# Turning one batch's normalised rows and folding the bias vectors in another way, in a gated attention kernel with experts

## What is computed

```python
qkv = jnp.einsum('bsh,oh->bso', hidden_states, w_qkv) + b_qkv
scores = jnp.einsum('bqh,bkh->bqk', q, k) / scaling
out = jnp.einsum('bsh,oh->bso', context, w_out) + b_out
...
logits = jnp.einsum('bsd,de->bse', x, router_w) + router_b
topk_vals, topk_idx = jax.lax.top_k(logits, TOP_K)
expert_out = jax.nn.silu(h)
out = jnp.einsum('bsd,df->bsf', combined, proj_w) + proj_b
return norm_w * (y / rms)
...
x = x + s * g
```

## Time and profile before

| | us |
|---|---|
| time, median of 3 runs | 485.66 (485.57 to 486.53) |
| the profiled execution's own time | 484.21 |
| its span, first to last instruction | 482.5 |
| TensorE busy in the span | 474.7 |
| VectorE, ScalarE, GpSimd busy | 315.7, 214.0, 217.6 |

### The profile page before, as it was taken

The page is one execution under the profiler, slowest core; times in us unless marked ns, Lnnn a source line. Parts: engine busy times, 40 slices in busy tenths (PEclk is TensorE's granted clock), DMA queues, the critical chain, the costliest instruction groups (busy, mean ns, idle before and its releaser), DMA issues.

```text
span 482.5 us, 7168 instructions
## 1 busy us (share of the span) xinstructions
PE 474.7 (98%) x2168; PEld 391.9 (81%) x2169; DVE 315.7 (65%) x471; ACT 214.0 (44%) x310; POOL 217.6 (45%) x318
## 2 busy tenths in 40 slices
PE   9999999999999999999999999999999999999995
PEld 7878777888888888888888888888888888888884
DVE  4965352776734446898888889753588665857653
ACT  3673563143230264644644444333655452554540
POOL 5685010007887859500400000664478873476234
PEclk9999999999999999999999999999999999999998
DMA  8956999956979599978789666996555874455412
GB/s 312 353 210 253 382 348 410 357 186 235 324 243 334 186 320 308 285 212 259 230 269 263 201 191 176 338 315 246 151 176 174 239 198 151 123 190 172 149 46 86
DMA packets 78192, 115.79 MB, mean 240 GB/s; under 512 B 6657, under 2 KB 36369, under 8 KB 78161
## 3 DMA queue, kind: packets, MB, share of 16 engines
q1 hardware_dynamic: 65072, 79.72, 52.5%
q0 software_dynamic: 6896, 23.36, 13.9%
q10 hardware_dynamic: 6192, 12.32, 7.3%
HBM read 66.09 MB, written 49.28 MB: 239 GB/s over the span
## 4 chain that ended last, share of the span: by engine, by line
PE 97%; DVE 1%; issue 1%; ACT 0%; DVEq 0%
PE ab L1662 22%; PE ab L1664 22%; PE ab L1663 22%; PE sc L1662 8%; PE sc L1664 7%; PE sc L1663 7%; PE tp L1668 2%; PE tp L1704 1%; PE tp L1763 1%; PE sc L1733 1%; PE sc L1774 1%; PE sc L1736 1%; PE ab L1686 0%; PE ab L1688 0%; DVE xt_l L1229 0%
## 5 line engine op out<-in xcount | busy, mean ns | idle before, releaser
L822 POOL DMA_INDIRECT y<-y_scratch,pos x32 | 33.3, 1042 | 77.7 <-DMA y_scratch<-yt_so 63.3
L1664 PE MATMUL ab<-W,st_l 128*128 x156 | 60.7, 389 | 0.0
L1663 PE MATMUL ab<-W,st_h 128*128 x156 | 60.7, 389 | 0.0
L1662 PE MATMUL ab<-W,st_h 128*128 x156 | 60.7, 389 | 0.0
L805 POOL DMA_INDIRECT rows_scratch<-xb,pos x32 | 31.2, 975 | 51.2 <-DVEq L1343 43.0
L1662 PE MATMUL sc<-xt_h,t_h 128*128 128x512 f32 x128 | 50.1, 391 | 0.0
L1664 PE MATMUL sc<-xt_h,t_l 128*128 128x512 f32 x128 | 49.9, 390 | 0.0
L1663 PE MATMUL sc<-xt_l,t_h 128*128 128x512 f32 x128 | 49.8, 389 | 0.0
L1081 ACT CAST st_h<-tp 128x512 fp32r<-128x512 f32 x39 | 22.9, 587 | 43.3 <-PE ab L1664 41.2
L1423 DVE TENSOR_REDUCE small<-sc 128x1 f32<-128x1024 f32 x16 | 19.5, 1221 | 24.7 <-PE sc L1664 24.4
L1664 PEld LDWEIGHTS ab<-W,st_l 128*128 128x128 f32 x156 | 29.3, 188 | 6.1
(11 more groups left out here) (286 smaller groups left out, 1227.4 us busy)
## 6 DMA issues: line engine op xcount, KB each, us to landing
rows_scratch<-xn ACTq DMA_DIRECT2D x3, 3328.0 KB, 20.1
xb<-in_expert_w POOLq DMA_DIRECT2D x6, 1024.0 KB, 10.1
xn<-rows_scratch SPq DMA_DIRECT2D x48, 128.0 KB, 3.1
xg<-rows_scratch SPq DMA_DIRECT2D x44, 128.0 KB, 3.1
y_scratch<-yt_own SPq DMA_DIRECT2D x20, 256.0 KB, 3.1
y_scratch<-yt_so SPq DMA_DIRECT2D x19, 256.0 KB, 3.1
p_scratch<-prob SPq DMA_DIRECT2D x9, 512.0 KB, 2.8
rows_scratch<-xs SPq DMA_DIRECT2D x16, 256.0 KB, 6.7
```

The lines of the kernel that those rows point to most:

```text
L822: pool.indirect_dma_start(y[:, q, :], None, y_d, bass.IndirectOffsetOnAxis(pos[:, GB * s + p:GB * s + p + 1], 0))\
L1662: nc.tensor.matmul(dst, lh, rh, start=start, stop=False)
L1663: nc.tensor.matmul(dst, lh, rl, start=False, stop=False)
L1664: return nc.tensor.matmul(dst, ll, rh, start=False, stop=stop)
```

## The change

Batch 1's rows are normalised in place (xb1), stay there for the scatter, and are stored to HBM as before. They aren't turned by TensorE: spread_pair, new on SP, waits for the stores of a pair and loads it back in four quarters, and turn_spread, new on VectorE, transposes blocks of 32 by 32 into tp. The scatter takes batch 1 first; eight loads to sent_rows are gone. The high and low halves of batch 1's last four tiles go to the room of the split key weights (turned_rows), so ScalarE waits with them until the folds are done. Two of the three clearing transfers are issued by SP behind spread_pair instead of by ScalarE. The expert weights' first loads wait for the last turn instead of the last normalised row, as they write the same buffer.

The bias vectors are made in another way: weigh_rows on VectorE adds up the rows of the query (key) weights, each chunk times its number of the other bias; GpSimd splits the sum in halves; sum_rows on TensorE multiplies a square of ones with both halves, so that every partition holds the whole vector; and pick on VectorE takes from it, with the identity, the number of each partition. The statistics of batch 1 are one turn earlier. The router's products of batch 0 now come ahead of those of batch 1.

```diff
...
+        def turned_rows(g):
+            w = slice(g % QB * P, (g % QB + 1) * P)
+            if g < GB:
+                return xt_h[:, :, g * P:(g + 1) * P], xt_l[:, :, g * P:(g + 1) * P]
+            if g < GB + QB:
+                return bt_h[:, :, w], bt_l[:, :, w]
+            return wk_h[:, :, w], wk_l[:, :, w]
...
-                sp.dma_start(rows_g[home(g)], xs[:, g % 4, :]).then_inc(xn_st[g % 4], 16)
+                sp.dma_start(rows_g[home(g)], xs[:, g % 4, :] if g < GB else xb1[:, g - GB, :])\
+                    .then_inc(xn_st[g % 4], 16)
+            def spread_pair(n):
+                g = GB + 2 * n
+                for k in (g, g + 1):
+                    sp.wait_ge(xn_st[k % 4], 16 * (k // 4 + 1))
+                for a in range(4):
+                    sp.dma_start(xb[32 * a:32 * (a + 1), 2 * n:2 * n + 2, :].rearrange("p t (r f) -> p (t r) f", r=4),
+                                 rows_q[home(g):home(g) + 2, a, :, :, :].rearrange("t s r f -> s (t r) f"))\
+                        .then_inc(x_in[n], 16)
             load_half(0)
-            for g in range(G):
+            for g in range(GB):
                 if g == 4:
                     load_half(1)
                 store_row(g)
+            for g in range(GB, GB + 4):
+                store_row(g)
+            for n in range(KC):
+                spread_pair(n)
+                if n < 2:
+                    store_row(GB + 4 + 2 * n)
+                    store_row(GB + 5 + 2 * n)
+            for n in (1, 2):
+                clear_slots(sp, n)
...
             def load_to_send(g):
-                if g >= GB:
-                    sp.wait_ge(sent[g % GB], 32)
-                sp.dma_start(sent_rows[:, g % GB, :], rows_g[home(g)]).then_inc(send_in[g % GB], 16)
+                sp.wait_ge(sent[g], 32)
+                sp.dma_start(sent_rows[:, g, :], rows_g[home(g)]).then_inc(send_in[g], 16)
...
+            link(pool.tensor_copy(ones_r[:, :], ones[:, :]))
+            for m in range(2):
+                pool.wait_ge(weighed, m + 1)
+                link(pool.tensor_copy(sums[m][:, 0, :], raw[m][:, 0, :]))
+                pool.tensor_tensor(sums[m][:, 1, :], raw[m][:, 0, :], sums[m][:, 0, :], ALU.subtract).then_inc(qk_split, 1)
+            pool.wait_ge(t_done, G)
...
-            for g in range(G):
-                pool.wait_ge(send_in[g % GB], 16 * (g // GB + 1))
+            for n in range(G):
+                g = (n + GB) % G
+                if n >= GB:
+                    pool.wait_ge(send_in[g], 16)
...
-                nc.scalar.activation(xs[:, g % 4, :], xbs[g // GB][:, g % GB, :], ACT.Identity, bias=shift[:, g:g + 1],
+                whole = xbs[g // GB][:, g % GB, :]
+                nc.scalar.activation(xs[:, g % 4, :] if g < GB else whole, whole, ACT.Identity, bias=shift[:, g:g + 1],
...
+                if g >= GB + QB:
+                    act.wait_ge(fold, 2 * KC)
+                high = turned_rows(g)[0]
...
             act.wait_ge(ln_done, 3)
-            for g in range(GB, GB + 4):
+            for g in range(GB, GB + 6):
                 normalise(g)
             fold_high(KC)
-            act.wait_ge(vecs, 2)
-            nc.scalar.copy(bias_rows, ab[0:2, :, :].rearrange("p a n -> p (a n)")).then_inc(rows_out, 1)
+            normalise(GB + 6)
+            act.wait_ge(qk_split, 6)
             hi(GB)
+            normalise(GB + 7)
             hi(GB + 1)
             fold_high(KC + 1)
-            normalise(GB + 4)
-            normalise(GB + 5)
             hi(GB + 2)
             hi(GB + 3)
             fold_high(KC + 2)
-            normalise(GB + 6)
-            normalise(GB + 7)
             fold_high(KC + 3)
-            act.wait_ge(rt_done, 1)
...
+            def weigh_rows(m):
+                other = bcols[:, 1 - m, :]
+                dve.wait_ge(qk_split, 4)
+                total = raw[m][:, 0, :]
+                link(vec.tensor_scalar(total, total, other[:, 0:1], None, ALU.mult))
+                for c in range(1, KC - 1):
+                    link(vec.scalar_tensor_tensor(total, raw[m][:, c, :], other[:, c:c + 1], total, ALU.mult, ALU.add))
+                vec.scalar_tensor_tensor(total, raw[m][:, KC - 1, :], other[:, KC - 1:KC], total, ALU.mult, ALU.add)\
+                    .then_inc(weighed, 1)
...
+            def turn_spread(g):
+                k = g - GB
+                dve.wait_ge(x_in[k // 2], 64 + 16 * (2 if k < 4 else 1))
+                dve.wait_ge(lo_done, g - 1)
+                vec.transpose(tp[:, g % 2, :, :].rearrange("p c (r s) -> p c r s", r=4),
+                              xb[:, k, :].rearrange("p (r q c) -> p c r q", r=4, c=KC)).then_inc(t_done, 1)
...
+            def pick(m, out):
+                each = picked[m].rearrange("p (c q) -> p c q", c=KC)
+                link(vec.tensor_tensor(each, ab[:, m, :].rearrange("p (q c) -> p c q", c=KC),
+                                       ident[:, :].unsqueeze(1).to_broadcast([P, KC, P]), ALU.mult))
+                return vec.tensor_reduce(out, each, AX.X, ALU.add)
...
+            def fold_query_bias():
                 dve.wait_ge(const, 6)
-                dve.wait_ge(vecs, 3)
-                two = lambda m: ab[:, 0, 2 * KC * m:2 * KC * (m + 1)].rearrange("p (c a) -> p c a", a=2)
-                vec.tensor_reduce(tb[:, :], two(0), AX.X, ALU.add).then_inc(pre_done, 1)
-                link(vec.tensor_reduce(rw[:, :, E], two(1), AX.X, ALU.add))
-                vec.tensor_reduce(rb_bc[:, E:E + 1], ab[:, 0, 4 * KC:5 * KC], AX.X, ALU.add).then_inc(pre_done, 1)
+                dve.wait_ge(vecs, 2)
+                link(vec.tensor_reduce(rb_bc[:, E:E + 1], ab[:, 1, 0:KC], AX.X, ALU.add))
+                pick(0, rw[:, :, E]).then_inc(pre_done, 1)
+                dve.wait_ge(pre_done, 2)
                 link(vec.tensor_copy(rw_hl[:, :, 0, :], rw[:, :, :]))
                 vec.tensor_tensor(rw_hl[:, :, 1, :], rw[:, :, :], rw_hl[:, :, 0, :], ALU.subtract).then_inc(pre_done, 1)
+            def fold_key_bias():
+                dve.wait_ge(vecs, 3)
+                pick(1, tb[:, :]).then_inc(pre_done, 1)
                 dve.wait_ge(pre_done, 4)
...
-                if 2 <= t < 6:
-                    n = t - 2
+                if 1 <= t < 5:
+                    n = t - 1
...
+            weigh_rows(0)
+            weigh_rows(1)
+            turn_spread(GB)
+            turn_spread(GB + 1)
             fold_low(KC)
             lo(GB)
+            turn_spread(GB + 2)
             lo(GB + 1)
+            turn_spread(GB + 3)
+            fold_query_bias()
             fold_low(KC + 1)
-            fold_biases()
             lo(GB + 2)
+            turn_spread(GB + 4)
             lo(GB + 3)
+            turn_spread(GB + 5)
             fold_low(KC + 2)
+            fold_key_bias()
             fold_low(KC + 3)
-            for g in range(GB + QB, G):
-                lo(g)
+            lo(GB + 4)
+            turn_spread(GB + 6)
+            lo(GB + 5)
+            turn_spread(GB + 7)
+            lo(GB + 6)
+            lo(GB + 7)
...
-            def bias_products():
-                for m, (high, low) in enumerate(((wk_h, wk_l), (wq_h, wq_l))):
-                    nc.tensor.matmul(ab[0:2, m, :], bc_hl[:, m, 0, :], high[:, 0, :], start=True, stop=False)
-                    for c in range(KC):
-                        nc.tensor.matmul(ab[0:1, m, :], bc_hl[:, m, c, 0:1], low[:, c, :], start=False, stop=False)
-                    for c in range(1, KC):
-                        last = nc.tensor.matmul(ab[0:2, m, :], bc_hl[:, m, c, :], high[:, c, :],
-                                                start=False, stop=(c == KC - 1))
-                last.then_inc(vecs, 1)
-            def turn_biases():
-                pe.wait_ge(rows_out, 1)
-                for n in range(2 * KC):
-                    nc.tensor.transpose(ab[:, 0, 2 * n:2 * n + 2], 
-                                        every_fourth(bias_rows[:, n // KC * D:(n // KC + 1) * D], n % KC), ident[0:2, 0:2])
-                nc.tensor.matmul(ab[:, 0, 4 * KC:5 * KC], ones[:, :], prod, start=True, stop=True).then_inc(vecs, 1)
...
+            def sum_rows(m):
+                pe.wait_ge(qk_split, 5 + m)
+                if m == 0:
+                    pe.wait_ge(ab_read, 2 + GB)
+                    nc.tensor.matmul(ab[:, 1, 0:KC], ones[:, :], prod, start=True, stop=True)
+                else:
+                    pe.wait_ge(pre_done, 2)
+                nc.tensor.matmul(ab[:, m, :], ones_r[:, :], sums[m][:, 0, :], start=True, stop=False)
+                nc.tensor.matmul(ab[:, m, :], ones_r[:, :], sums[m][:, 1, :], start=False, stop=True).then_inc(vecs, 1)
...
             pe.wait_ge(qk_split, 4)
             pe.wait_ge(pre_done, 1)
             fold_keys(FOLDS[0])
-            pe.wait_ge(ab_read, 2 + GB)
-            bias_products()
-            turn(GB)
-            turn(GB + 1)
             fold_keys(FOLDS[1])
-            turn_biases()
-            turn(GB + 2)
```

(17 more changed lines are left out.)

64 lines of the change are left out of this document (31 added, 33 removed).

## The result

| | kernel before | changed kernel |
|---|---|---|
| median (lowest to highest), us | 485.62 (485.23 to 486.53) | 490.12 (489.43 to 490.44) |
| ratio, 95% interval | | 1.0081 (1.0065 to 1.0097) |
| profiled execution, its span, granted clock | 484.21, 482.5, 0.997 | 489.43, 487.7, 0.989 |

The changed kernel is slower by 4.5 us by the medians and by 3.9 us by the ratio; the forecast was 3.8 us slower, 489.5. The spans of the two profiled executions differ by 5.2, and all of that is made in one stretch. The first fold starts at 45.99 (45.97 before); the scores start at 91.36 instead of 86.16; the attention's first product comes 22.4 us behind the scores in both kernels.

A forecast was written before the change was run, and what follows sets the result against it. TensorE's instruction row was taken as the bound: 8.0 us less work against 10.7 of waiting gave +2.65, the clock's fall added 1.1, so +3.8 on 485.66, 489.5 us; range 485.0 to 493.0.

The forecast's parts named there:

- 8.0 saved, 10.7 of waiting: TensorE before the scores: 8.0 us net less work against 10.7 us of new waits, scores 2.65 us later.
- The half of the turns: TensorE's four pairs of row-tile turns before the scores, about 1.05 us a pair, 4.2 us of work removed.
- the half of the bias vectors: TensorE's bias products (3.69 us) and bias-row turns with ones product (1.3) go; new products cost 1.2.
- T: Time the first pair of batch 1's rows is back from HBM: 56.7, bounds 54.8 and 61.6.
- The weighted sums: VectorE's two row sums from 47.5, 3.0 us each, done at 50.5 and 53.5; TensorE waits 0.8.
- The pick: VectorE's first bias pick, queued behind transposes, ends 8.4 us after T; TensorE idles 9.1 us until 65.1.
- The clock: Granted clock halves in TensorE's long wait; slow products behind it cost 2.0 us, adding 1.1 net.
- The wait of 0.9 for the third fold's low half: TensorE, second half of the logits: waits 0.9 us for VectorE, which has 6.1 us queued against TensorE's 5.2.
- The backlog of transfers: Rival: queued transfers delay the first probabilities' store and load at the attention, 1 to 3 us more, 491.5; 9 in 100.
- the end moves by what the scores move by: Sign in the profile after: the span's end shifts by the same amount as the start of the scores.
- The hidden round trip: Rival: weighted sums hide the trip, transposes start at 53.5, Q 3.2 us sooner, time 485.3; 14 in 100.
- The steady clock: Rival: the clock holds through TensorE's idle time, all else as forecast, 488.3; 15 in 100.

The follow-up runs named there:

- e5: Changed kernel's trip of batch 1's rows through HBM alone, bias vectors made as in the kernel before: 489.91 us, ratio 1.0077 to the kernel before.
- e8: e7 with VectorE's key pick behind the last fold's low half and TensorE's wait for it moved to the attention's key products: 481.69 us, ratio 0.9917.
- e9: Changed kernel without the 16 loads in quarters, transposes reading the buffer as it stands (results wrong): 485.15 us, ratio 0.9986 to the kernel before.
- e3: Changed kernel with 36 unused products in TensorE's long wait to hold the clock up: 491.27 us, ratio 1.0114 to the kernel before.
- e6: e3 with the 2 MB store of folded key weights issued behind the fourth probabilities' load: 488.48 us, ratio 1.005 to the kernel before.
- e7: e4 with sums in VectorE's pauses, statistics earlier, clears moved, folds, turns and picks reordered, key weights' store late: 484.29 us, ratio 0.996.
- e10: Changed kernel with both halves reordered: picks and low halves ahead of transposes, TensorE's batch 1 work last, late key weights' store: 482.5 us, ratio 0.9923.
- e1: Changed kernel with the first bias pick moved directly behind the weighted sums, ahead of the block transposes: 489.76 us, ratio 1.0085 to the kernel before.
- e12: e11 with its second clear cut from 13 tiles to 7, the rest on SyncE behind the loads in quarters: 479.39 us, ratio 0.9876.
- e11: e10 with the first tile's maximum ahead of routing, choices counted later, second clear issued from ScalarE in turn 5: 483.33 us, ratio 0.9945.
- e4: Kernel before with the bias half alone, batch 1 still turned by TensorE, clears where they were: 484.15 us, ratio 0.9966.
- e2: Changed kernel with the first clearing transfer also issued behind the loads in quarters: 497.7 us, ratio 1.0227 to the kernel before.

## Why the prediction was right, and where not

The mechanism was right: the work that leaves TensorE is outweighed by one long wait for a pick that stands behind the round trip. That the time came out so close is in part luck, as the next paragraphs show: most sizes missed to the same side, the trace moved by 5.2 us where 3.8 were forecast, and the medians moved by less than the traces.

**The balance.** "8.0 saved, 10.7 of waiting" was the argument. Measured: 10.5 of waiting (1.06 and 9.44; forecast 0.8, 9.1, 0.9) and 2.2 for the clock. The stretch of 45.4 less 10.5 and 2.2 is 32.7, so the work is 7.5 less than in the 40.2 before, not 8.0. Forecast: -8.0 + 10.7 + 1.1 = +3.8, where the 1.1 are a clock's price of 2.0 less 0.9 of waiting under it; in the trace: -7.5 + 10.5 + 2.2 = +5.2. The half of the turns was worth 3.6 us of work in e5 (43.2 less 5.35 of waits and 1.3 of clock is 36.6, against 40.2), not 4.2, the half of the bias vectors 3.6 in e8, not 3.8. The 1.05 us for a pair of turns don't follow from its two terms either: 0.87 and 0.27 are 1.14.

**T, the end of the trip.** Forecast 56.7, measured 57.82. The stores were sized at landing by 52.2, and SP issued the loads at 53.79: this step was 1.6 us short, since they landed in 4.3 to 5.6 us. The loads, sized by their twin at 4.5, took 4.0. The second pair came 3.75 us behind the first and not 2.6, so it was 0.20 late for VectorE instead of well ahead. GpSimd's end at 46.1 (forecast 45.8) and ScalarE's start at 46.67 (forecast 46.8) held.

**The weighted sums.** Sized at 3.0 each; the second took 3.9, because two of its steps ran beside GpSimd's copy and subtraction and took 2.65 instead of 1.54. It ended at 54.1, not 53.5, inside the cover of the trip. The same slowed GpSimd and made the first wait 1.06 and not 0.8. I had priced each engine's steps alone.

**The pick.** Forecast 8.4 behind T, measured 8.3: the count of VectorE's queue was right, and e9, with the same 8.3 behind a start 3.6 us earlier, shows that it counts by itself.

**The clock.** Forecast 2.0, less 0.9 of cover. Products from 66.08 to 70.91 took 4.83 us for 11 x 0.235 = 2.59: 2.2. The wait of 0.9 for the third fold's low half lay under it, as assumed; with the clock held up it comes out, at 0.6 (e3, e6). The fall itself came 4.2 us behind TensorE's stop, where rows 15 give 2.4 (476.7 to 479.1, by the mean of 0.78). With 1.1 late at T, 0.1 early at the pick and 0.5 more behind it the scores are 1.4 later than forecast; the executions' medians differ by less than their traces (4.5 against 5.2), so the time came out only 0.6 above.

The rule of the Trainium skill ("TensorE: Matmul & The Clock Gate", section "HAM oscillation — how this bites in real kernels") that TensorE starts at the lower clock behind a long wait for a DMA held: the granted clock was 0.50 at 66.08, behind a wait for VectorE, which had itself waited for a DMA. By it the sum was +3.8, without it +2.65.

**Taken at nothing.** The backlog of transfers was ranked as a rival with 9 in 100. In the changed kernel it did nothing (22.4 us in both), but e3 shows how near it was: with the scores 1.3 us earlier the attention's first product waited 1.24. The statement that the end moves by what the scores move by held only because the wait covered the backlog, and that the moved clears are free holds for this kernel alone. Nor were the transfers idle between 53 and 64: their share was 0.86 or more from 56 to 66, at only 191 to 343 GB/s.

**The rivals.** The hidden round trip needs T of 53.5, which is 1.3 us below the lower bound of T, 54.8, and not half a microsecond; its 14 in 100 rest on that slip. e9 comes near that case (54.24) and gives 485.15 where 485.3 was worked out, but that is luck: the clock fell there too, and the eight slow products cost 1.6 us, not 0.2. The steady clock is e6: 488.48 where 488.3 was worked out, but only with the backlog shortened; with the clock alone (e3) the rival's figure would have been wrong by 3.

What stays open: why waits of nearly the same length in e7 and in e10 did and did not lower the clock (below), why it came back so late in e1, and how much of e12's gain is owed to each of its placements.

## What to carry to other kernels

Work taken off the busiest engine is worth what the slowest of the replacements lets through: list, on the engine that does the new work, everything that stands behind its wait for a transfer, and move ahead whatever doesn't need the data. A long wait hides other bounds just behind it, so a fix of that wait (e1) or of its price (e3) alone may gain nothing; look at what arrives next with little slack, and count the clock again for the wait that is left. When a store's latency matters, look at what bulk transfers are queued at the moment it is issued, and cut them to the idle time that is there.

## What the runs showed of the hardware

In the changed kernel the granted clock fell 4.2 us after TensorE stopped (56.5 to about 60.7) and came back 4.8 us after it went on (66.1 to 70.9); in e5 it fell 3.6 us after the stop at 65.1 and was back 2.8 us after work began at 69.2. In e9 these were 2.5 (from 56.65) and 3.4 us (from 62.51), in e1 4.4 (from 60.4) and 8.9 (from 66.15, with an idle time of 0.84 in between). So the fall came 2.5 to 4.4 us behind the stop and the return 2.8 to 8.9 us behind the restart, in one and the same stretch of a program. In the profiled execution of e7 a wait of 1.84 us went ahead of a fall, which came when TensorE had worked again for almost a microsecond. Waits of 2.0 us in e10 and 1.9 in e11 left it at 1.00. None of these runs tells what the difference is.

A weighted step of VectorE on two SBUF operands took 0.75 us by itself, 0.98 and 1.64 beside GpSimd's copy and subtraction in the changed kernel, which took 0.73 instead of 0.61 and 1.59 instead of 1.28; GpSimd's small steps went from 0.20 to as much as 0.73 in e4.

At the same place of the program, four stores of 256 KB landed in 2.0 to 2.1 us with no clear under way (e2), in 2.9 to 3.9 where the last clear landed 1.7 us behind the first store's issue (e12), in 4.3 to 5.6 where it landed 3.6 us behind it (the changed kernel), and in 6.8 to 7.7 where it landed 8.6 us behind it (e11).
